# Layer 2's masked attention: the key chunks of blocks 10 and 12, and the place of the rows' turns in block 13

## The reference, cut to what matters

```
xn = layernorm(x)                                # 8 x 256 x 128, the "rows"
q = (xn @ Wq + bq) / 8     16 heads of 64        # 256 x 64 per head
k = ctx @ Wk + bk          16 heads of 64        # 1601 x 64 per head
v = ctx @ Wv + bv          16 heads of 64
attn = softmax(where(mask, q @ k.T, -1e30))      # 256 x 1601 per head
x = x + (attn @ v) @ Wo + bo
```

## Time and profile before

| what | value |
|---|---|
| median of 3 runs | 4399.22 us (4398.59 to 4399.37) |
| the profiled execution's own time | 4397.88 us |
| its span, first to last instruction | 4396.1 us |
| mean granted TensorE clock | 0.962 |
| PE busy over the span | 4091.0 us (93%) |
| PEld / ACT / DVE / POOL busy | 67% / 64% / 63% / 19% |
| DMA, mean over the span | 18 GB/s |
| layer 2's attention, stretch 1229 to 2824 us | 1595 us, PE busy 1545.87, ACT 1075.87, DVE 948.07 |

### The profile page before, as it was taken

One profiled execution on the slowest core, in us unless ns is written; L12 is line 12 of the kernel. 1 busy time (PEld: TensorE's weight loads), 2 busy tenths in 40 slices (PEclk: granted clock), 3 DMA queues, 4 the chain that ended last, 5 costly groups with the idle time before them and its releaser, 6 DMA issues. The chain is left out here.

```text
span 4396.1 us, 73213 instructions
## 1 busy us (share of the span) xinstructions
PE 4091.0 (93%) x26955; PEld 2930.5 (67%) x26988; DVE 2771.0 (63%) x6291; ACT 2799.0 (64%) x4880; POOL 826.0 (19%) x727
## 2 busy tenths in 40 slices
PE   7897999999889999999999999789999999989799
PEld 6654454454467777777777777547888888865467
DVE  7655888888465656565656565465555555548656
ACT  6523667767356667676767666537777777756456
POOL 2100000000000000000000000006777777751100
PEclk9898999999899999999999999889999999988899
DMA  2101433221100000000000000100000000000100
GB/s 67 44 1 30 76 45 49 38 43 20 44 13 1 12 12 1 12 1 12 1 12 4 9 1 1 42 16 8 8 9 8 9 1 1 1 9 1 40 3 8
DMA packets 79677, 78.97 MB, mean 18 GB/s; under 512 B 10372, under 2 KB 72996, under 8 KB 78220
## 3 DMA queue, kind: packets, MB, share of 16 engines
q1 hardware_dynamic: 74860, 67.97, 7.4%
q10 hardware_dynamic: 4464, 6.30, 0.4%
HBM read 51.31 MB, written 4.19 MB: 13 GB/s over the span
## 5 line engine op out<-in xcount | busy, mean ns | idle before, releaser
L2439 POOL TENSOR_TENSOR L3a_p_lo<-L3a_wq,L3a_p_hi 128x512 fp32r<-128x512 f32 (+1 forms) x480 | 621.3, 1305 | 264.0 <-ACT L3a_p_hi L2389 256.4
L1287 DVE CUSTOM_DVE_ANT_0 L2a_sc<-L2a_score,L2a_mask_n 128x804 f32<-128x804 f32 x512 | 498.9, 991 | 223.1 <-issue 196.4
L1190 ACT ACTIVATE L2a_pt<-L2a_ring 128x512 f32<-128x512 f32 x768 | 431.1, 598 | 174.5 <-PE L2a_ring L1076 169.9
L631 ACT ACTIVATE L1a_work<-L1a_ring 128x1024 f32<-128x1024 f32 x416 | 412.8, 1026 | 162.6 <-PE L1a_ring L449 162.3
L752 DVE TENSOR_REDUCE L1a_mx<-L1a_ring 128x2 f32<-128x1024 f32 x384 | 456.4, 1222 | 57.3 <-PE L1a_ring L468 52.2
L1076 PE MATMUL L2a_ring<-L2a_ident,L2a_sc 128*128 128x128 f32 x3072 | 437.1, 280 | 5.9 <-ACT L2a_sc L1175 1.9
L1175 ACT ACTIVATE L2a_sc<-L2a_sc,L2a_nb 128x1608 f32<-128x1608 f32 x256 | 417.3, 1632 | 0.7 <-DVE L2a_nb L1292 0.7
L2527 DVE TENSOR_REDUCE L3a_mx<-L3a_ring 128x1 f32<-128x402 f32 (+2 forms) x640 | 316.5, 538 | 144.6 <-PE L3a_ring L2241 137.1
L1076 PEld LDWEIGHTS L2a_ring<-L2a_ident,L2a_sc 128*128 128x128 f32 x3072 | 343.6, 142 | 79.7 <-issue 42.1
L2388 ACT ACTIVATE L3a_wq<-L3a_ring 128x512 f32<-128x512 f32 (+1 forms) x480 | 283.5, 591 | 159.2 <-PE L3a_ring L2163 102.2
L1091 PE MATMUL L2a_res<-L2a_pt,L2a_v 128*64 128x256 f32 (+1 forms) x3328 | 373.4, 381 | 1.7 <-ACT L2a_pt L1190 1.7
(11 more groups left out here) (749 smaller groups left out, 9067.0 us busy)
## 6 DMA issues: line engine op xcount, KB each, us to landing
L1a_keys<-L1a_k_hi SPq DMA_DIRECT2D x224, 52.0 KB
L1a_cx<-in_ctx SPq DMA_DIRECT2D x8, 768.0 KB
L2a_cx<-in_ctx SPq DMA_DIRECT2D x8, 768.0 KB
L1a_keys<-L1a_k_lo SPq DMA_DIRECT2D x112, 52.0 KB
L0a_cx<-in_ctx SPq DMA_DIRECT2D x16, 320.0 KB, 3.7
L3a_cx<-in_ctx SPq DMA_DIRECT2D x16, 320.0 KB, 3.4
L2a_mask_u<-in_mask SPq DMA_DIRECT2D x16, 200.1 KB, 4.7
L1a_scr_q<-L1a_keys SPq DMA_DIRECT2D x3, 1024.0 KB
```

The costliest lines, as they stand in the source:

```text
L631: act.activation(probs[:, (par * NU + u) % c.PS, :, :], ring[tile][:, :, :], ACT.Exp).then_inc(tile_free[tile], 1)
L1190: ins = act.activation(pt[:, t:t + 4, g // 3, q], bank[:, :].rearrange("p (t q) -> p t q", t=4), ACT.Copy)
L1287: dve.tensor_tensor_reduce(sc[:, two, e, w].rearrange("p (k j) -> p k j", k=2), score[e][:, :, 0:CH], mask_n[:, r % 2, w].rearrange("p (k ...
L2439: pool.tensor_tensor(p_lo[0:r, at % PL, 0:W], probs[0:r, at % 2, 0:W], p_hi[0:r, at % PH, 0:W].bitcast(F32), ALU.subtract).then_inc(part_o ...
```

## The change

Three edits, all in layer 2's attention.

1. A new method `upto` gives blocks 10 and 12 a table of their own in place of the even spread: `query` stands at the first of the ten places, ahead of the two `max`, `key 0` at the fifth, between them and `scores(r, 1)`, and `key 1` at the last.
2. In block 13 the two `turn_x` come before the last two `turn_c`.
3. As `turn_x` is no longer the last of these, the one-off work on ACT (wv_hi, and the sum of biases) moves from `turn_x` to the last `turn_c`.

```diff
         if r == 13:
-            return keys + [("turn_c", k, 1) for k in range(self.KB)] + [("turn_x", hf, 1) for hf in range(SH)]
+            turns = [("turn_c", k, 1) for k in range(self.KB)]
+            return keys + turns[0:2] + [("turn_x", hf, 1) for hf in range(SH)] + turns[2:]
...
+    def upto(self, r, k, tasks):
+        places = 5 if r % 2 else 10
+        if r in (10, 12):
+            return (0, 1, 1, 1, 1, 2, 2, 2, 2, 2, 3)[k]
+        return k * tasks // places
...
         some = lambda *ks: [put(kind, n, at) for k in ks
-                            for kind, n, at in tasks[k * len(tasks) // places:(k + 1) * len(tasks) // places]]
+                            for kind, n, at in tasks[self.upto(r, k, len(tasks)):self.upto(r, k + 1, len(tasks))]]
...
             def turn_c(b, par, k):                 # ACT
                 act.activation(kt_hi[:, w], bank[:, 0:w.stop - w.start], ACT.Copy).then_inc(hi_ok, 1)
+                if isinstance(b, int) and b == 0 and k == KB - 1:
+                    act.activation(wv_hi[:, :], wv, ACT.Copy).then_inc(w_hi_ok, 1)
+                    act.wait_ge(bias_mm, 1)
+                    act.activation(bfin[:, :], res[:, 0:1], ACT.Identity, bias=bo[:, 0:1], scale=1.0).then_inc(bias_ok, 1)
...
             def turn_x(b, par, hf):                # ACT
-                if isinstance(b, int) and b == 0 and hf == SH - 1:
-                    act.activation(wv_hi[:, :], wv, ACT.Copy).then_inc(w_hi_ok, 1)
-                    act.wait_ge(bias_mm, 1)
-                    act.activation(bfin[:, :], res[:, 0:1], ACT.Identity, bias=bo[:, 0:1], scale=1.0).then_inc(bias_ok, 1)
```

More of the change, by code:

```diff
@@ L837, in slot @@
         tasks = self.beside(r)
-        places = 5 if odd else 10
         some = lambda *ks: [put(kind, n, at) for k in ks
-                            for kind, n, at in tasks[k * len(tasks) // places:(k + 1) * len(tasks) // places]]
+                            for kind, n, at in tasks[self.upto(r, k, len(tasks)):self.upto(r, k + 1, len(tasks))]]
         turn = lambda *gs: [put("turn", (prev, g), off) for g in gs]
```

## The result

The changed kernel takes 4425.9 us (median of 6 runs, 4419.2 to 4434.23), the kernel before 4398.91 us beside it (6 runs, 4396.04 to 4400.63). The ratio is 1.0063, 95% interval 1.0051 to 1.0076: slower by 27 us, and clear of noise. Timed again later, the same kernel stood at 4432.09 against 4395.97 us (1.0075, 1.0062 to 1.0089). The forecast was 4432, with 4415 to 4446 as its range.

The account below looks back on a forecast made before the run. PE, busy 93% of the span, was taken to bound the kernel, so a new order changes only waits and clock. 23.7 + 9.3 + 1.1 - 1.0 = +33.1 on the median 4399.22 gave 4432 us, range 4415 to 4446.

Parts of the forecast that it names:

- q_lo ahead of both `max`: Blocks 10 and 12: both `max` stand behind q_lo on DVE, which needs ACT's q_hi, so `scores(r, 1)` starts 1.78 us later.
- Key 0 inside the wait, then `values` waiting for ACT: Blocks 10 and 12: key 0 fills 0.66 us, `values` waits about 0.33 for ACT; 16 x 1.48 = +23.7 us.
- rival C: Blocks 10 and 12: `values` finds ACT done, +27 in all, 4427 us; chance 0.13.
- The clock: Blocks 10 and 12: falls behind 12 of 16 waits, 1.0 us each, less 2.7 for two earlier falls: +9.3 us.
- Rival A: Blocks 10 and 12: the clock holds, +21.1 us in all, 4420 us; chance 0.17.
- Rival B: Blocks 10 and 12: the clock falls behind all 16 waits at full price, +42.6 us in all, 4442 us; chance 0.09.
- Block 13: `turn_x` wait of 0.65 goes, the second turn of block 14 waits on kt_lo instead; seven passages, +1.1 us.
- Rival 1 of that part: From the theory for edits 2 and 3 alone: the wait saved at `turn_x` counts, -5.7 us, 4393 us; no chance given.
- Before the first batch: Once: wv_hi comes earlier on ACT, so the first value matmul's 1.88 us wait goes, about 1 us lost elsewhere: -1.0 us.
- Rival D: Blocks 10 and 12: q_lo costs DVE no wait and key 0 fills PE's idle time, -14 us, 4385 us; chance 0.03.

Follow-up runs that it names:

- the query alone: Against the kernel before, only query moved ahead of both `max` in blocks 10 and 12, key chunks and block 13 as before: 4439.47 us, ratio 1.0105.
- The filled wait: Changed kernel, but PE computes key 0 of pairs 6 and 7 four times over into the same tile: 4412.9 us, ratio 1.0038 to the kernel before.
- the run of edits 2 and 3: Against the kernel before, `turn_x` ahead of the last two `turn_c` and the one-off ACT work moved, blocks 10 and 12 as before: 4394.58 us, ratio 1.0002.
- Block 13 in pairs: Kernel before with key 0 between the scores and, in block 13, turn_x(0), turn_c(2) ahead of the exp, turn_x(1), turn_c(3) behind: 4384.84 us, ratio 0.9969.
- the key alone: Against the kernel before, only key 0 of blocks 10 and 12 moved between the two scores, query behind both `max`: 4379.2 us, ratio 0.9969; again 4380.97 us.

## Why the prediction was right

- **q_lo ahead of both `max`.** It was to delay `scores` by 1.78 us. Measured from the query matmul, 3.73 us against 1.94, so 1.79. The run with the query alone shows that nothing else in edit 1 costs.
- **Key 0 inside the wait, then `values` waiting for ACT.** Forecast 1.48 per block, measured 1.50 (24.43 to 24.48 against 22.94 and 22.97). From the last key chunk to `values` it is 0.98 us where a chunk takes 0.66, the 0.33 that was forecast. That refutes rival C, by which `values` would not wait. (By the prediction's own terms PE arrives at 1757.96 and not at 1757.99; the 1.48 doesn't rest on it.)
- **The clock.** The term of +9.3 came out as +11.3 in the profiled execution, but by luck, as a product of two wrong factors: 8 falls and not 12, and 1.35 (block 10) or 2.42 us (block 12) each and not 1.0. The reason given for the low price, that a fall which begins while PE still waits costs less than 1.34, is the wrong way round: those are the falls that cost 2.42. So the pairs reached 26.93 us where "up to 25.8" was the sign to look for. In the other two profiled executions with the same wait the count was 8 and 13. The filled wait shows the cause, PE's idle time; the count can't be forecast from one trace. Rival A, a clock that holds, was refuted in every profiled execution with the long wait, and with it, as far as waits of 2.5 us go, the rule of the Trainium skill's page "TensorE: Matmul & The Clock Gate" (section "HAM oscillation — how this bites in real kernels"), by which only longer idle stretches cost the array its clock: the measurement decides, and it shows falls. Rival B fell too: never did all 16 waits have a fall behind them, 13 at most.
- **Block 13.** The 0.65 at turn_x went and 0.49 came at the second turn of block 14; the pair is 26.13, 0.14 over the usual 25.99, where 0.16 was worked out. The prediction's sign was a wait of about 0.7 there; it is 0.49, though the turn starts when it was forecast to, 12.43 us behind the end of block 12's `values`. Rival 1 of that part, a gain of 5.7, is refuted by the run of edits 2 and 3, where the pair is longer and not shorter. The prediction read kt_lo before the change as standing behind the second `max`; that names only one of two that ended together, the other is ACT's kt_hi (see "Block 13 in pairs"). Its sum doesn't rest on this, the theory of that later run did.
- **Before the first batch.** -0.8 for a forecast -1.0: from PE's first matmul of the stage to the end of the first `values` it is 52.28 us in the changed kernel and 53.04 before. The other traces agree, 52.2 to 52.4 in the three others with edits 2 and 3 as they are, 53.0 to 53.1 in the five with block 13 as before.
- **Rival D**, faster because the key fills idle time, names the right effect of the wrong edit: the key without the query gives it, at 4379 us.
- The sum, +33.1, lies between the two measured differences, +27 and +36. The terms that it names measure 24.0 + 11.3 + 0.6 - 0.8 = +35.1 in the profiled executions; the falls elsewhere, which it doesn't name, took 9.0 back there. That the median came as near as it did is in part luck: the fastest and slowest runs of the changed kernel lie 15 us apart, those of the filled wait 7.

## What to carry to other kernels

A step that is written out once for all engines moves in every engine's queue: before it is moved to fill PE's gap, ask what DVE and ACT will now do first, and whether its input is there by then. A subtraction of 0.4 us ahead of the row maxima cost 1.8, of which 1.3 was DVE waiting with its real work at hand. Where a matmul engine waits in one long piece, count the clock as well, and give it other work of the same kind if there is any. Even useless work paid here against the same order without it, though it didn't make that order a good one: it is still 17 us slower than the kernel before.

## What the runs showed of the hardware

- Nine redundant matmuls in each of 16 waits made the kernel 19 us faster (4412.9 against 4432.09), through the clock: no falls in the 16 pairs against 8, and those 8 cost 13.7 us in one execution. The pairs at full clock are as long as without the extra matmuls.
- PE idle for 2.5 us in one piece let the clock fall to 1.2 GHz behind 8 to 13 of 16 such waits, and 3.0 us behind 11 of 16; with PE's longest wait there at 0.7 us (the key alone, two traces) none of 16 had a fall, and with a single wait of 1.24 us (block 10 of the kernel before and of edits 2 and 3) none of 8. How often it falls behind one and the same wait also changes with edits elsewhere: the wait of block 12 as it was before had a fall in two of eight batches, and in six with edits 2 and 3.
- A fall that began while PE still waited lasted about twice as long as one that began when it was back at work, and cost 2.42 us and not 1.35 (changed kernel).
